# Layer 0 attention: the mixing of one group of heads moved ahead of the scores of a later group in TensorE's order

## The chip, the core and the metric

The kernel runs on one core of one Trainium2 chip. The core has five engines that each work through their own list of instructions in order and meet at semaphores: TensorE (PE in the profile; its weight loads are shown apart as PEld), VectorE (DVE), ScalarE (ACT), GpSimd (POOL) and SyncE (SP), which only starts transfers. The metric is the device time of one execution in microseconds: the median of three runs.

## The reference

The program is a stack of four layers of attention and experts over `x` of 8 sequences x 128 tokens x 256 features. The change touches only the attention of layer 0. What it computes:

```python
ln_out = _ln(hidden_states, ln_w, ln_b)
q  = _ln(fp8_linear(ln_out, wq,  ...))      # 16 heads of 128, self attention
k  = _ln(fp8_linear(ln_out, wk,  ...))      #  8 heads
v  =     fp8_linear(ln_out, wv,  ...)
core = _gqa(q, k, v)
qx = _ln(fp8_linear(ln_out, wqx, ...))      # 16 heads, cross attention
kx, vx = split(cond @ w_kv_x.T); kx = _ln(kx)
xout = _gqa(qx, kx, vx)
catq = _div_clamp_fp8(concatenate([core, xout]), proj_smooth)
out  = catq @ wproj.T * (proj_in_scale * proj_w_scale)

def _gqa(q, k, v):                          # each key head serves two query heads
    scores = einsum('bsghd,btgd->bghst', q, k) / sqrt(128)
    return einsum('bghst,btgd->bsghd', softmax(scores), v)
```

Here `_ln` is a normalisation over the 128 features of a head, and `_div_clamp_fp8` rounds to the values of an 8-bit float. Everything else of the four layers stays as it is.

## The kernel before

`layer0_attention` does the work in two passes over the 8 sequences, 16 tiles in all (`b` from 0 to 15): tiles 0 to 7 are the cross attention, tiles 8 to 15 the self attention. A tile has 8 units of work in the order k0, q0, k1, q1, v0, q2, v1, q3. A unit is 512 columns, that is four heads. The four units q0 to q3 (`a` from 0 to 3) each become one *group*: scores, softmax and mixing of four heads. So there are 64 groups.

A unit passes through a chain of small steps on four engines: `project` on TensorE (L456 for keys and values of the first pass, L466 for all others), squares on ScalarE (L818), their sum on VectorE (L666), the power -1/2 on GpSimd (L948), the product on VectorE (L674, `normalise`), `turn` on TensorE (L475, four transposes), and the copy of the turned block with scale and bias on ScalarE (L832 writes `q_t`, L837 writes `k_t`). A group then goes on: `score` on TensorE (L484, reads `q_t` and `k_t`), `row_max` on VectorE (L679), exponentials on ScalarE (L846), inverse of the row sum on VectorE (L683), `scale_probs` on ScalarE (L890), `turn_probs` on TensorE (L492), `keep_probs` on ScalarE (L853, writes `probs_t`), `mix` on TensorE (L501, reads `probs_t` and `values`), `round_mixed` on VectorE (L689, L638 to L644) and GpSimd (L920, L924, writes `cat`), `project_out` on TensorE (L512). ScalarE's copy of v into `values` is L824.

The order in which an engine does all this is written out by `march` (L163). Time is cut into steps, eight to a tile, and each function has a list of steps at which it is due, relative to its tile; a late due time reaches into the next tile. In each step `march` runs through its list of functions in the order of the list and calls those that are due. So the list sets the order within a step, and every engine has its own list. The lists are the whole plan: nothing else decides what stands behind what.

On TensorE `score` is due 4 steps and `mix` 8 steps behind the projection of its unit. Query units are at steps 1, 3, 5 and 7, so both fall on odd steps, and the two of one step belong to different groups: with the scores of group n goes the mixing of group n-2. On ScalarE, in the even step before, `keep_turned` (L832) writes the `q_t` that these scores need, and directly behind it `keep_probs` (L853) writes the `probs_t` that this mixing needs.

Of the kernel before, what the change touches and what calls it, by code (L numbers as in the profile page):

```python
# [162 lines left out]
def march(vts, steps, work):  # L163

    last = max(s for _, due in work for s in due)
    for g in range(vts * steps + last):
        for function, due in work:
            for k, s in enumerate(due):
                b, left = divmod(g - s, steps)
                if left == 0 and 0 <= b < vts:  # L170
                    function(b, k)
# [19 lines left out]
def layer0_attention(nc, top, res, w, before):  # L191


    PASSES, VTS = 2, 2 * TILES
    UNITS = [("k", 0), ("q", 0), ("k", 1), ("q", 1), ("v", 0), ("q", 2), ("v", 1), ("q", 3)]
    STEPS = len(UNITS)
# [8 lines left out]
    with phase_memory(nc, "l0a", res.given_back) as mem:  # L205
# [114 lines left out]
        at_norm, at_plain, at_query = NORMED, PLAIN, QUERY  # L320

        def later(due, n):
            return [s + n for s in due]
# [7 lines left out]
        F_TILE = VTS - 1  # L331
        F_ROWS_TILE, F_ROWS = VTS - 2, [8, 11, 12]
        F_TURN = [12, 13]
# [3 lines left out]
        def in_tile(tile, function, due):  # L337
            def at_step(b, k):
                if b == tile:
                    function(k)  # L340
            return at_step, due
# [49 lines left out]
        def _(pe):  # L391
# [136 lines left out]
            def first_up(k):  # L528
# [9 lines left out]
                for c in range(KC):  # L538
# [1 line left out]
                                   start=(c == 0), stop=(c == KC - 1))  # L540
                mm.then_inc(res.first_up_made, 1)

            march(VTS, STEPS, [(turn_probs, later(at_query, 7)), (score, later(at_query, 4)),
                               (mix, later(at_query, 8)), in_tile(F_TILE, turn_first, F_TURN),
                               in_tile(F_TILE, first_up, F_UP), (project_out, later(at_query, 11)),
                               (turn, later(at_norm, 3)), (project, range(STEPS)),
                               in_tile(0, centre_first, [0]), in_tile(0, centre_next, [1, 3, 5])])
# [2 lines left out]
        def _(v):  # L550
# [142 lines left out]
            def add_to_x(b, _):  # L693
                projected_out.wait(v, projected_out.at(b, NA))
                xt = res.x[:, b % TILES, :]
                v.scalar_tensor_tensor(xt, out_bank[:, 0:D], out_scale[:, 0:1], xt, ALU.mult, ALU.add)\
                 .then_inc(x_done.sem, 1)
                if b >= TILES:
                    token_moments(v, res, res.x, [b - TILES])
# [210 lines left out]
        def _(g):  # L910
# [60 lines left out]
            def first_rstd(_):  # L971
                g.wait_ge(f_var_ready, 1)
                g.tensor_tensor(f_rstd[:], f_var[:], res.minus_half[:, 0:4], ALU.pow).then_inc(f_rstd_ready, 1)
# [2789 lines left out]
```

## Time and profile before

| | |
|---|---|
| median of 3 runs | 1504.31 us (1501.78 to 1506.41) |
| the profiled execution | 1502.7 us |
| its span | 1500.9 us |
| PE, PEld, DVE, ACT, POOL busy in the span | 96%, 69%, 58%, 51%, 35% |
| granted TensorE clock, mean | 0.994 of full speed |

The span is the time from the first to the last instruction of the profiled execution; 1.8 us of its time lie around it. Busy time is the sum of the instructions of an engine. The ends of matmuls are modelled, so PE's busy share tells little of whether it had to wait; the idle time ahead of its weight loads (PEld) tells more. In a timeline row the columns are start, duration, engine, line, operation, output and inputs with their shapes, the number of instructions merged in the row, and in brackets the idle time of that engine just before and who ended it. The layer 0 attention takes the span from about 32 us to about 461 us.

### The profile page before, as it was taken

To read this page: it belongs to the slowest core of one execution; us is meant where nothing else is said; L and a number is where in the kernel's file an instruction comes from. 1 tells how busy PE (TensorE), PEld (TensorE's weight loads), DVE (VectorE), ACT (ScalarE), POOL (GpSimd) and SP (SyncE) were. 2 spreads that over 40 slices of the span, in tenths; PEclk is the share of its full clock that TensorE was granted. 3 is DMA by queue.
4 is the path that set the end of the run, shared out by engine and by line. 5 is a ranking of instruction groups with operands and counts; after the bars stand their busy time and mean duration, and the time that the engine had idled before them with its cause. 6 is when DMAs were issued, how large, how long until landed. Compare 5 with 4: busy or idle time off the path is not lost. (4 is left out here: it accounts for less than half of the span.)

```text
span 1500.9 us, 22370 instructions
## 1 busy us (share of the span) xinstructions
PE 1437.8 (96%) x7006; PEld 1040.2 (69%) x7006; DVE 877.0 (58%) x1923; ACT 768.6 (51%) x2123; POOL 526.4 (35%) x522
## 2 busy tenths in 40 slices
PE   6999999999989999999999999999997999999998
PEld 5677777788875555557878888866764666665656
DVE  5798988899875242333464545455677555553322
ACT  5888888999982211110234444444357655553210
POOL 2767677877761000000533333322111333321000
PEclk9999999999999999999999999999999999999999
DMA  5301000200006511112100000000232000011120
GB/s 204 118 6 64 5 5 1 97 1 1 2 1 265 180 53 49 49 50 91 67 1 1 0 1 1 15 15 6 102 150 97 1 1 1 1 30 43 47 69 17
DMA packets 21880, 71.67 MB, mean 48 GB/s; under 512 B 3922, under 2 KB 6354, under 8 KB 19076
## 3 DMA queue, kind: packets, MB, share of 16 engines
q1 hardware_dynamic: 13556, 57.38, 10.4%
q10 hardware_dynamic: 8208, 12.87, 2.8%
q8 instruction: 58, 0.95, 0.3%
q14 instruction: 58, 0.48, 0.1%
HBM read 69.01 MB, written 1.22 MB: 47 GB/s over the span
## 5 line engine op out<-in xcount | busy, mean ns | idle before, releaser
L1282 ACT ACTIVATE l0f_silu<-bank 128x512 f32<-128x512 f32 x48 | 28.5, 597 | 198.9 <-PE bank L1206 183.0
L948 POOL TENSOR_TENSOR l0a_head_rstd<-l0a_head_var,all_minus_half 128x4 f32<-128x4 f32 x96 | 99.6, 1042 | 18.2 <-DVE l0a_head_var L666 18.2
L1385 DVE TENSOR_TENSOR l0f_product<-l0f_silu,bank 128x512 f32<-128x512 f32 x48 | 32.9, 687 | 124.3 <-ACT l0f_silu L1282 124.2
L920 POOL TENSOR_TENSOR l0a_stepped<-l0a_y,l0a_m 128x512 f32<-128x512 bf16 x64 | 73.8, 1153 | 89.1 <-DVE l0a_m L644 87.5
L484 PEld LDWEIGHTS bank<-l0a_k_t,l0a_q_t 128*128 128x128 f32 x512 | 63.7, 191 | 39.7 <-ACT l0a_q_t L832 35.3
L846 ACT ACTIVATE l0a_work<-bank,l0a_neg_max 128x128 f32<-128x128 f32 x256 | 90.3, 372 | 1.2 <-DVE l0a_neg_max L679 1.2
L1218 PEld LDWEIGHTS bank<-all_weights_a,l0f_hidden 128*128 128x128 f32 x384 | 72.9, 190 | 25.3 <-issue 17.0
L1814 DVE TENSOR_TENSOR all_weights_a<-bank,all_cols 128x512 f32<-128x512 f32 x64 | 43.9, 690 | 77.6 <-PE bank L1649 46.2
L1218 PE MATMUL bank<-all_weights_a,l0f_hidden 128*128 128x256 f32 x384 | 88.9, 379 | 0.0
L2407 PE MATMUL bank<-l3a_f_xn_t,all_weights_b 128*128 128x512 f32 x192 | 86.2, 594 | 0.0
L890 ACT ACTIVATE l0a_work<-l0a_work,l0a_row_inv 128x128 f32<-128x128 f32 x256 | 82.4, 411 | 6.2 <-DVE l0a_row_inv L683 5.9
L924 POOL TENSOR_TENSOR l0a_cat<-l0a_stepped,l0a_m 128x512 fp32r<-128x512 f32 x64 | 79.3, 1239 | 10.2 <-issue 7.9
L484 PE MATMUL bank<-l0a_k_t,l0a_q_t 128*128 128x128 f32 x512 | 71.6, 283 | 9.4 <-ACT l0a_q_t L832 8.7
L1997 ACT ACTIVATE l1a_work<-bank,l1a_exp_bias,l1a_q_scale 128x128 f32<-128x128 f32 x128 | 56.8, 454 | 41.9 <-DVE l1a_exp_bias L1880 41.9
L2713 POOL TENSOR_TENSOR l3a_probs<-l3a_probs,l3a_row_inv 128x512 f32<-128x512 f32 x32 | 33.3, 1039 | 126.6 <-DVE l3a_row_inv L2514 126.6
L674 DVE TENSOR_TENSOR l0a_work<-bank,l0a_head_rstd 128x512 f32<-128x512 f32 x96 | 65.1, 678 | 16.0 <-POOL l0a_head_rstd L948 15.8
L666 DVE TENSOR_REDUCE l0a_head_var<-l0a_squares 128x4 f32<-128x516 f32 x96 | 65.6, 683 | 7.5 <-ACT l0a_squares L818 6.3
L818 ACT ACTIVATE l0a_squares<-bank 128x512 f32<-128x512 f32 x96 | 58.0, 604 | 23.1 <-DVE l0a_head_var L666 14.6
L512 PE MATMUL bank<-l0a_wp_high,l0a_cat 128*128 128x256 f32 x256 | 69.4, 305 | 0.0
L475 PE MATMUL bank<-all_ident,l0a_work 128*128 128x128 f32 x384 | 59.0, 276 | 8.3 <-DVE l0a_work L674 8.1
L501 PE MATMUL bank<-l0a_probs_t,l0a_values 128*128 128x256 f32 x256 | 66.0, 380 | 0.2 <-ACT l0a_probs_t L853 0.2
L512 PE MATMUL bank<-l0a_wp_low,l0a_cat 128*128 128x256 f32 x256 | 63.6, 281 | 0.0
(443 smaller groups left out, 3760.3 us busy)
## 6 DMA issues: line engine op xcount, KB each, us to landing
l0f_spread<-l0f_weights ACTq DMA_DIRECT2D x32, 192.0 KB, 2.7
all_weights_a<-in_l_w_q SPq DMA_DIRECT2D x2, 2048.0 KB, 13.8
l0f_spread<-l0f_weights ACTq DMA_DIRECT2D x32, 128.0 KB, 2.8
all_weights_b<-in_l_e_gate_up SPq DMA_DIRECT2D x1, 3200.0 KB, 10.4
all_weights_b<-in_l_e_gate SPq DMA_DIRECT2D x1, 3072.0 KB, 10.0
all_weights_a<-in_l_e_up SPq DMA_DIRECT2D x4, 768.0 KB, 6.7
all_weights_a<-in_l_e_down SPq DMA_DIRECT2D x1, 3072.0 KB, 15.2
l3a_spread<-l3f_weights SPq DMA_DIRECT2D x10, 256.0 KB, 3.4
```

What stands on the lines that cost most here:

```text
L484: mm = pe.matmul(score_bank[:, h * P:(h + 1) * P], q_t[:, h * P:(h + 1) * P], k_t[:, a // 2, g * P:(g + 1) * P], start=True, stop=True)
L501: mm = pe.matmul(mix_bank[:, half * 2 * P:(half + 1) * 2 * P], values[:, a // 2, g * P:(g + 1) * P], probs_t[:, half * 2 * P:(half + 1) * ...
L512: mm = pe.matmul(out_bank[:, 0:D], cat[:, a % 2, h * P:(h + 1) * P], part[:, a * HU + h, :], start=(a == 0 and h == 0 and n == 0), stop=(a ...
L666: v.tensor_reduce(head_var[:, m % 2, :], squares[:], X, ALU.add).then_inc(var_ready.sem, 1)
L674: v.tensor_tensor(heads(norm_rows[:, m % 2, :]), heads(bank_of(b, NORMED[n])), along(head_rstd[:, m % 2, :], P), ALU.mult).then_inc(norm_d ...
L846: done = act.activation(probs[:, a % 2, h * P:(h + 1) * P], score_bank[:, h * P:(h + 1) * P], ACT.Exp, bias=neg_max[:, a, h:h + 1], accum_ ...
L890: done = act.activation(pr, pr, ACT.Copy, scale=row_inv[:, a, h:h + 1])
L920: done = g.tensor_tensor(stepped[:, 0:n], value, step, ALU.add)
L924: return g.tensor_tensor(out, stepped[:, 0:n], step, ALU.subtract)
L948: g.tensor_tensor(head_rstd[:, m % 2, :], head_var[:, m % 2, :], res.minus_half[:, 0:HU], ALU.pow)\
L1218: mm = pe.matmul(down_banks[t // 2][:, (t % 2) * D:(t % 2 + 1) * D], hidden[:, n % 2, t * P:(t + 1) * P], w_down[:, j, :], start=(j == 0 a ...
L2407: mm = pe.matmul(bank[:], w_gate_up[:, c, i * (NCH - 1) * P + col:i * (NCH - 1) * P + col + P], f_xn_t[:, c, h * HALF:(h + 1) * HALF], sta ...
```

## The change

In TensorE's list the entry for `mix` stands ahead of that for `score`, where it stood behind it:

```diff
-            march(VTS, STEPS, [(turn_probs, later(at_query, 7)), (score, later(at_query, 4)),
-                               (mix, later(at_query, 8)), in_tile(F_TILE, turn_first, F_TURN),
+            march(VTS, STEPS, [(turn_probs, later(at_query, 7)), (mix, later(at_query, 8)),
+                               (score, later(at_query, 4)), in_tile(F_TILE, turn_first, F_TURN),
                                in_tile(F_TILE, first_up, F_UP), (project_out, later(at_query, 11)),
                                (turn, later(at_norm, 3)), (project, range(STEPS)),
```

No instruction is added or removed, no due step changes, and the lists of the other engines are the same.

On TensorE, in a step of the first pass in which a key block is turned as well (L456 is a projection of the cross attention, L484 the scores, L501 the mixing, L475 the turn, L466 a projection of queries):

```order
 L456 MATMUL bank<-l0a_wkx,l0a_ctx_t 128x512 [waits l0a_kx_ready,l0a_ctx_in,l0a_norm_done]
 L456 MATMUL bank<-l0a_wkx,l0a_ctx_t 128x512
-L484 MATMUL bank<-l0a_k_t,l0a_q_t 128x128 [waits l0a_exp_done,l0a_turned_out]
-L484 MATMUL bank<-l0a_k_t,l0a_q_t 128x128 x3
-L501 MATMUL bank<-l0a_probs_t,l0a_values 128x256 [waits l0a_mixed_read,l0a_values_done,l0a_probs_t_ready]
-L501 MATMUL bank<-l0a_probs_t,l0a_values 128x256
+L501 MATMUL bank<-l0a_probs_t,l0a_values 128x256 [waits l0a_mixed_read,l0a_values_done,l0a_probs_t_ready]
+L501 MATMUL bank<-l0a_probs_t,l0a_values 128x256
+L484 MATMUL bank<-l0a_k_t,l0a_q_t 128x128 [waits l0a_exp_done,l0a_turned_out]
+L484 MATMUL bank<-l0a_k_t,l0a_q_t 128x128 x3
 L475 MATMUL bank<-all_ident,l0a_work 128x128 [waits l0a_turned_out,l0a_norm_done]
 L475 MATMUL bank<-all_ident,l0a_work 128x128 x3
```

The two mixing matmuls, with their wait for `probs_t`, moved ahead of the four of the scores, with their wait for `q_t`. The turn and the projection keep their places behind the pair.

On TensorE, in a step of the second pass in which no key block is turned:

```order
 L466 MATMUL bank<-l0a_wk_high,l0a_xq 128x512
 L466 MATMUL bank<-l0a_wk_low,l0a_xq 128x512
-L484 MATMUL bank<-l0a_k_t,l0a_q_t 128x128 [waits l0a_exp_done,l0a_turned_out]
-L484 MATMUL bank<-l0a_k_t,l0a_q_t 128x128 x3
-L501 MATMUL bank<-l0a_probs_t,l0a_values 128x256 [waits l0a_mixed_read,l0a_values_done,l0a_probs_t_ready]
-L501 MATMUL bank<-l0a_probs_t,l0a_values 128x256
+L501 MATMUL bank<-l0a_probs_t,l0a_values 128x256 [waits l0a_mixed_read,l0a_values_done,l0a_probs_t_ready]
+L501 MATMUL bank<-l0a_probs_t,l0a_values 128x256
+L484 MATMUL bank<-l0a_k_t,l0a_q_t 128x128 [waits l0a_exp_done,l0a_turned_out]
+L484 MATMUL bank<-l0a_k_t,l0a_q_t 128x128 x3
 L466 MATMUL bank<-l0a_wq_high,l0a_xq 128x512 [waits l0a_w_low,l0a_quant_done,l0a_values_done]
 L466 MATMUL bank<-l0a_wq_low,l0a_xq 128x512
```

The same swap; here the query projection stands directly behind the pair. It occurs in 62 places in all: the first two groups of scores have no mixing beside them, and the last two mixings no scores.

On ScalarE, whose order is the same in both kernels, an even step and the odd step behind it (L846 exponentials, L832 `q_t`, L853 `probs_t`, L890 the scaling of the probabilities, L824 `values`, L818 squares):

```order
L846 ACTIVATE l0a_work,l0a_row_sum<-bank,l0a_neg_max 128x128 x3
L832 ACTIVATE l0a_q_t<-bank,l0a_q_affine 128x512 [waits l0a_scored,l0a_turned]
L853 ACTIVATE l0a_probs_t<-bank 128x512 [waits l0a_mixed,l0a_probs_turned]
L890 ACTIVATE l0a_work<-l0a_work,l0a_row_inv 128x128 [waits l0a_inv_ready]
L890 ACTIVATE l0a_work<-l0a_work,l0a_row_inv 128x128 x3
L824 ACTIVATE l0a_values<-bank 128x512 [waits l0a_mixed,l0a_projected]
L818 ACTIVATE l0a_squares<-bank 128x4x128 [waits l0a_var_ready,l0a_projected]
```

What TensorE's mixing waits for (L853) is written directly behind what its scores wait for (L832).

## Rows read from the trace of the kernel before

**Rows 1.** The page, part 1: busy us, share of the span, instructions.
```profile
PE 1437.8 (96%) x7006; PEld 1040.2 (69%) x7006; DVE 877.0 (58%) x1923; ACT 768.6 (51%) x2123; POOL 526.4 (35%) x522
```

**Rows 2.** Windows, second pass: span, PE, PEld, DVE, ACT, POOL, clock, DMA, GB/s.
```profile
299.00:400.00 101.00, 97.92 (x618) 82.53 (x617) 91.15 (x194) 92.72 (x296) 77.94 (x81) 1.00 0.01 1
```

**Rows 3.** Waits of TensorE's weight loads, first pass: us, times, longest.
```profile
PEld bank L484 <- ACT l0a_q_t L832: 21.3, 32, 2.6
PEld bank L484 <- issue: 3.8, 16, 0.2
```

**Rows 4.** The same view, 245 to 456 us, second pass.
```profile
PEld bank L484 <- ACT l0a_q_t L832: 14.0, 26, 1.2
```

**Rows 5.** Timeline, first pass, a group whose scores find their input ready.
```profile
139.06 0.80 ACT L832 ACTIVATE l0a_q_t<-bank,l0a_q_affine 128x512 f32<-128x512 f32 x1
...
139.72 0.62 ACT L853 ACTIVATE l0a_probs_t<-bank 128x512 f32<-128x512 f32 x1
140.12 0.19 PEld L484 LDWEIGHTS bank<-l0a_k_t,l0a_q_t 128*128 128x128 f32 x1 [0.24 <-ACT l0a_q_t L832]
...
140.55 0.86 PEld L484 LDWEIGHTS bank<-l0a_k_t,l0a_q_t 128*128 128x128 f32 x7 [0.24 <-issue]
...
141.33 0.73 PEld L501 LDWEIGHTS bank<-l0a_probs_t,l0a_values 128*128 128x128 f32 x4
```

**Rows 6.** Timeline, first pass, a group whose scores wait.
```profile
100.39 0.79 ACT L832 ACTIVATE l0a_q_t<-bank,l0a_q_affine 128x512 f32<-128x512 f32 x1
...
101.05 0.61 ACT L853 ACTIVATE l0a_probs_t<-bank 128x512 f32<-128x512 f32 x1
101.23 0.63 PEld L484 LDWEIGHTS bank<-l0a_k_t,l0a_q_t 128*128 128x128 f32 x5 [1.25 <-ACT l0a_q_t L832]
```

**Rows 7.** Timeline, ScalarE, first pass, between two `q_t`.
```profile
149.23 0.60 ACT L824 ACTIVATE l0a_values<-bank 128x512 f32<-128x512 f32 x1 [1.05 <-PE bank L501]
150.09 0.60 ACT L818 ACTIVATE l0a_squares<-bank 128x512 f32<-128x512 f32 x1 [0.27 <-PE bank L466]
```

**Rows 8.** Waits, 32 to 456 us, of ScalarE's copy of v.
```profile
ACT l0a_values L824 <- PE bank L501: 6.9, 8, 1.1
```

**Rows 9.** Timeline, TensorE's weight loads, one tile of the second pass.
```profile
350.79 0.97 PEld L484 LDWEIGHTS bank<-l0a_k_t,l0a_q_t 128*128 128x128 f32 x8 [0.64 <-ACT l0a_q_t L832]
...
355.31 0.46 PEld L475 LDWEIGHTS bank<-all_ident,l0a_work 128*128 128x128 f32 x4
...
361.30 0.42 PEld L475 LDWEIGHTS bank<-all_ident,l0a_work 128*128 128x128 f32 x4 [0.23 <-DVE l0a_work L674]
363.04 1.09 PEld L484 LDWEIGHTS bank<-l0a_k_t,l0a_q_t 128*128 128x128 f32 x8
...
367.71 0.42 PEld L475 LDWEIGHTS bank<-all_ident,l0a_work 128*128 128x128 f32 x4 [0.40 <-DVE l0a_work L674]
...
373.90 0.42 PEld L475 LDWEIGHTS bank<-all_ident,l0a_work 128*128 128x128 f32 x4
375.68 0.41 PEld L484 LDWEIGHTS bank<-l0a_k_t,l0a_q_t 128*128 128x128 f32 x3 [0.62 <-ACT l0a_q_t L832]
```

**Rows 10.** Timeline, ScalarE, the same tile.
```profile
356.09 0.80 ACT L832 ACTIVATE l0a_q_t<-bank,l0a_q_affine 128x512 f32<-128x512 f32 x1
...
362.00 0.78 ACT L832 ACTIVATE l0a_q_t<-bank,l0a_q_affine 128x512 f32<-128x512 f32 x1
362.68 0.59 ACT L853 ACTIVATE l0a_probs_t<-bank 128x512 f32<-128x512 f32 x1
...
374.83 0.80 ACT L832 ACTIVATE l0a_q_t<-bank,l0a_q_affine 128x512 f32<-128x512 f32 x1
```

**Rows 11.** Timeline, VectorE: a row maximum of the same tile, then the stage's end.
```profile
353.62 0.68 DVE L679 TENSOR_REDUCE l0a_neg_max<-bank 128x4 f32<-128x512 f32 x1
...
434.88 0.69 DVE L679 TENSOR_REDUCE l0a_neg_max<-bank 128x4 f32<-128x512 f32 x1 [1.43 <-PE bank L484]
436.42 0.69 DVE L674 TENSOR_TENSOR l0a_work<-bank,l0a_head_rstd 128x512 f32<-128x512 f32 x1 [0.85 <-POOL l0a_head_rstd L948]
```

## The prediction

> **What bounds the kernel now.** I read the page first. TensorE is busy for 96% of the span, far ahead of the others [rows 1], but the ends of its matmuls are modelled, so this does not say that it never waits. I read therefore the waits of its weight loads, in each half of the layer 0 attention. What it waits for there is above all one thing: the scores (L484) wait for `q_t`, 32 times and 21.3 us in the first pass [rows 3], 26 times and 14.0 us in the second [rows 4]. The mixing (L501) is no entry of that size: it always came behind the scores, and its input was there. The reader should see that the change moves exactly these two.
>
> Then I took single groups from the timeline. In the first pass they are of two kinds. In 16 groups the array is still at work when the scores' first weights are loaded: the load at 140.12 is followed by the second only at 140.55, after 0.24 us of "issue" [rows 5], and the waits view counts 16 such gaps [rows 3]. TensorE is the late one here. In the others (32 less 16, less the first two groups, which have no mixing: 14) TensorE stands idle, 1.25 us at 101.23 [rows 6], until `q_t` is written. ScalarE, which writes it, had itself waited for TensorE before: 1.05 us for the mixing and 0.27 us for the projection of the same step [rows 7]. So TensorE and ScalarE form a ring, with no slack in it. In the second pass VectorE (91.15 of 101 us) and ScalarE (92.72 of 101 us) are nearly full as well [rows 2], and TensorE also waits for VectorE's `l0a_work` ahead of two turns of a tile, 0.23 and 0.40 us [rows 9]. There is slack there.
>
> **The change, part by part.** Nothing is added or removed; 62 pairs are swapped. Three things follow.
>
> First, TensorE now stops for `probs_t` instead of `q_t`, and everything behind it in its queue (scores, turn, projection, the next transposes, `project_out`) waits too. ScalarE writes `probs_t` directly behind `q_t`: `q_t` ends at 100.39 + 0.79 = 101.18, the scores' load starts at 101.23, and `probs_t` ends at 101.05 + 0.61 = 101.66 [rows 6]. With the same 0.05 us behind it the mixing starts at 101.71: **0.48 us more idle time**. In a group of the first kind `probs_t` ends at 139.72 + 0.62 = 140.34; the mixing's load could start at 140.39 and its matmul some 0.11 us later (seven loads of the scores take 0.86 us in rows 5, so 0.12 each), at 140.50, while the array is busy until 140.55 [rows 5]. **It pays nothing.** In the six groups of the second pass that do not wait, `probs_t` ends at 362.68 + 0.59 = 363.27 [rows 10], against a load at 363.04 [rows 9]: 0.28 us later, less 0.12 us by which that group's loads were held up by the busy array (1.09 against 0.97 us for the eight loads), so **0.16 us**.
>
> Second, the scores end later still, by the mixing ahead of them: 0.73 us of loads [rows 5], together about 1.2 us. VectorE takes the row maximum 353.62 - (350.79 + 0.97) = 1.9 us behind the last load of the scores, of which some 0.2 us is the last matmul [rows 9, 11]: 1.7 us of slack cover the 1.2 us in the steady second pass. I count nothing there. At the end of the stage the cover is gone: VectorE itself waits 1.43 us for the scores at 434.88, and the next thing it does waits 0.85 us for GpSimd [rows 11]. So of 1.2 us between 0.35 and 1.2 are paid once by the last groups. I take 1.0, because behind the very last scores hardly anything else is left to hide them.
>
> Third, the mixing ends 0.4 us earlier than now (0.48 us later start, but 0.9 us of scores no longer ahead). Eight times ScalarE's copy of v waits for it, 6.9 us in all [rows 8]. But directly behind the copy ScalarE waits again, for the projection that stands behind both [rows 7], and that one comes later, not earlier. So this gain turns into a longer wait one instruction on: nothing.
>
> A rule of the Trainium skill would soften the first point. The trace first: in the 1.25 us of idle time at 101.23 no weight load of the work behind (mixing, projection) went ahead of the waiting scores [rows 6]; TensorE's loads stood still. "TensorE: Matmul & The Clock Gate", in the section on what each phase is for, says that TensorE's queue may pull a weight load ahead of matmuls in flight. By that rule the first load of the scores could be done while the mixing waits, and by the trace it cannot; the rival below has the price.
>
> The sum. First pass: 14 groups pay 0.48 us. Since ScalarE's last wait before such a group is for TensorE [rows 7], a delay of TensorE comes back with the next `q_t`, and the payments add up. I leave out the first of them, at the filling of the stage, where ScalarE is the late one: 13 x 0.48 = **6.2 us**. Second pass: a tile lasts 375.68 - 350.79 = 24.89 us [rows 9] and pays 3 x 0.48 + 0.16 = 1.6 us. Against this stand the slacks of its four turns: 0.23 and 0.40 us of waiting for VectorE [rows 9], and the time from turn to `q_t`, which is 0.70 us where ScalarE waits for the turn (361.30 to 362.00), 0.78 at 355.31 and 0.93 at 373.90, so 0.08 and 0.23 us [rows 9, 10]. 1.6 less 0.94 leaves 0.66; I take 0.6 us a tile, and four tiles of this even kind (from 300 to 400 us). In the tiles before and behind them TensorE's waits for VectorE are longer and swallow it. **2.4 us.** The end of the stage: **1.0 us.** Together 9.6 us. The stages behind start from the end of this one and are only shifted. The profiled execution of 1502.7 us becomes 1512.3; it lies 1.6 us below the median, and the median of 1504.31 becomes **1514**.
>
> Bounds: nothing at all if each delay falls into slack (1504), and from above every group in full: 14 + 26 groups at 0.48, 16 + 6 at 0.28 (the later load, whatever the array does), and 1.2 at the end, together 26.6 us (1531). The value taken lies nearer the lower end because the 16 groups are held by the busy array and the second pass by VectorE.
>
> **The rivals.**
> *It is hidden (no change).* VectorE and ScalarE are over 90% busy in the second pass [rows 2] and TensorE has slack there; if the first pass behaves so too, the delays never close the ring. It speaks against it that ScalarE waits for TensorE right before the waits of TensorE [rows 7]. The 2.4 us go and the 6.2 us shrink to less than half: 1504 to 1508. Chance 0.12.
> *Every delay is paid, and late scores cost too.* VectorE falls behind at the row maxima, its lateness comes back through `l0a_work` to the turns, and the slack at the two turns is no more. For it speaks that VectorE is as full as ScalarE; against it the 1.7 us of cover. Between the forecast's 9.6 and 26.6 us, near the upper end: about 1526. Chance 0.13.
> *Faster.* The place is ScalarE's copy of v: with the mixing 0.4 us earlier in 8 groups, and the mixed heads earlier at `round_mixed`, the ring loses 8 x 0.4 = 3.2 us, at most the 6.9 us [rows 8]. It decides only if ScalarE's next wait, for the projection, were not behind it; that is in the trace [rows 7]. 1497 to 1501. Chance 0.03.
> *TensorE loads ahead.* If weights of the scores are loaded while the mixing waits, each paying group gives back one load, 0.12 us of its 0.48: a quarter of the 8.6 us of both passes, 2.2 us, 1512. This is the mechanism of the page named above. Chance 0.04.
>
> **How the numbers follow.** The forecast has 0.68 and a range of its own from 1509 to 1519: the first pass alone, with two or three of its groups absorbed, gives 5 us, and one us more for each of the four tiles gives 13.6. The whole range takes in most of the no-change and part of the full-payment case: 1507 to 1523. A difference under 0.3% (4.5 us) cannot be told from no change. Faster by more than that: 0.02 (the upper half of that rival). Within 0.3%: the hidden case and the lower half of the faster one, with a little of the forecast's lower edge, 0.13. Slower: 0.85.
>
> **What would show it.** Right: TensorE's waits at L484 for `q_t` vanish, and waits at L501 for ScalarE's L853 stand in their place, some 40 of them and about 0.5 us longer each; the loads at L501 start 0.05 us behind the end of L853; ScalarE's wait at L824 for L501 shrinks and the one behind it at L818 grows. The period of a tile grows by 1 to 2 us around 90 to 115 us, by 0.5 to 0.7 us from 300 to 400 us, and not where TensorE is late throughout (139 to 153 us). The stage ends about 10 us later and all behind is shifted unchanged. Wrong: `probs_t` ready before TensorE arrives in most groups (then the change costs nothing), or VectorE waiting at L679 in the steady tiles (then it costs more), or the difference lying outside layer 0's attention.

## The result and the profile after

The changed kernel takes **1514.02 us** (median of 5 runs, 1509.39 to 1516.63), the kernel before 1504.31 us (median of 5 runs beside them, 1501.78 to 1506.41): ratio 1.0066, 95% interval 1.0043 to 1.0089, so slower by 6.5 to 13.4 us. Forecast were 1514 us and slower. The profiled execution took 1515.11 us, with a span of 1513.3 us.

Part 1 of the page after, beside [rows 1], tells next to nothing: every engine does the same work.

```profile
PE 1437.7 (95%) x7004; PEld 1041.7 (69%) x7006; DVE 876.5 (58%) x1923; ACT 766.7 (51%) x2123; POOL 526.1 (35%) x522
```

The waits of TensorE's weight loads after, 32 to 466 us (waited for, us in total, times, longest), answer to [rows 3, 4]:

```profile
PEld bank L501 <- ACT l0a_probs_t L853: 59.9, 63, 1.9
...
PEld bank L484 <- ACT l0a_q_t L832: 3.8, 2, 2.6
PEld bank L475 <- DVE l0a_work L674: 3.7, 8, 1.1
```

The wait for `q_t` is gone but for the first two groups, which have no mixing beside them. The wait for `probs_t` stands in its place, in 63 of the 64 mixings. The same view for the engines around:

```profile
DVE l0a_neg_max L679 <- PE bank L484: 24.9, 29, 2.8
ACT l0a_squares L818 <- PE bank L466: 24.0, 30, 1.4
...
ACT l0a_values L824 <- PE bank L501: 0.8, 5, 0.2
```

ScalarE's wait at its copy of v shrank from 6.9 us [rows 8] to 0.8. Its wait at the squares rose to 24.0 us; the view of the kernel before, 32 to 456 us, has for the two entries that grew:

```profile
ACT l0a_squares L818 <- PE bank L466: 4.8, 19, 0.3
...
DVE l0a_neg_max L679 <- PE bank L484: 3.9, 3, 1.7
```

The pair of [rows 7] after, ScalarE between two `q_t` of the first pass. The wait moved one instruction on, from the copy to the squares:

```profile
151.72 0.60 ACT L824 ACTIVATE l0a_values<-bank 128x512 f32<-128x512 f32 x1 [0.16 <-PE bank L501]
153.48 0.60 ACT L818 ACTIVATE l0a_squares<-bank 128x512 f32<-128x512 f32 x1 [1.16 <-PE bank L466]
```

Now the single groups. The one of [rows 6] after, ScalarE:

```profile
101.84 0.80 ACT L832 ACTIVATE l0a_q_t<-bank,l0a_q_affine 128x512 f32<-128x512 f32 x1
...
102.50 0.62 ACT L853 ACTIVATE l0a_probs_t<-bank 128x512 f32<-128x512 f32 x1
```

and TensorE's loads:

```profile
103.17 0.73 PEld L501 LDWEIGHTS bank<-l0a_probs_t,l0a_values 128*128 128x128 f32 x4 [1.60 <-ACT l0a_probs_t L853]
103.92 1.08 PEld L484 LDWEIGHTS bank<-l0a_k_t,l0a_q_t 128*128 128x128 f32 x8
```

The mixing's load starts at 103.17, which is 0.05 us behind the end of `probs_t` (102.50 + 0.62). Measured from the start of `q_t`, TensorE goes on 1.33 us later (103.17 - 101.84), where it was 101.23 - 100.39 = 0.84: 0.49 us, as predicted (0.48). The matmuls of the same two places, before (first fence) and after (second), show the idle time of the array itself, which is shorter than that of the loads (1.25 and 1.60 us). Their ends are modelled, so these figures are rough:

```profile
101.23 1.16 PE L484 MATMUL bank<-l0a_k_t,l0a_q_t 128*128 128x128 f32 x8 [0.42 <-ACT l0a_q_t L832]
```
```profile
103.17 1.13 PE L501 MATMUL bank<-l0a_probs_t,l0a_values 128*128 128x256 f32 x4 [0.77 <-ACT l0a_probs_t L853]
```

The group of [rows 5], where the array was late, after:

```profile
142.45 0.80 ACT L832 ACTIVATE l0a_q_t<-bank,l0a_q_affine 128x512 f32<-128x512 f32 x1
...
143.12 0.62 ACT L853 ACTIVATE l0a_probs_t<-bank 128x512 f32<-128x512 f32 x1
...
143.79 0.77 PEld L501 LDWEIGHTS bank<-l0a_probs_t,l0a_values 128*128 128x128 f32 x4 [0.52 <-ACT l0a_probs_t L853]
...
143.93 1.03 PE L501 MATMUL bank<-l0a_probs_t,l0a_values 128*128 128x256 f32 x4
```

The profile puts 0.52 us of waiting down here, and yet nothing is lost: the load at 143.79 precedes the matmul by 0.14 us, because the array is still at work. An idle time of the loads is not yet an idle time of the array.

One tile of the second pass after, beside [rows 9, 10]. ScalarE:

```profile
356.80 0.80 ACT L832 ACTIVATE l0a_q_t<-bank,l0a_q_affine 128x512 f32<-128x512 f32 x1
357.47 0.62 ACT L853 ACTIVATE l0a_probs_t<-bank 128x512 f32<-128x512 f32 x1
...
382.43 0.80 ACT L832 ACTIVATE l0a_q_t<-bank,l0a_q_affine 128x512 f32<-128x512 f32 x1
```

TensorE's loads:

```profile
358.14 0.73 PEld L501 LDWEIGHTS bank<-l0a_probs_t,l0a_values 128*128 128x128 f32 x4 [0.90 <-ACT l0a_probs_t L853]
358.89 1.08 PEld L484 LDWEIGHTS bank<-l0a_k_t,l0a_q_t 128*128 128x128 f32 x8
...
362.65 0.46 PEld L475 LDWEIGHTS bank<-all_ident,l0a_work 128*128 128x128 f32 x4
...
368.85 0.46 PEld L475 LDWEIGHTS bank<-all_ident,l0a_work 128*128 128x128 f32 x4
```

The tile lasts 382.43 - 356.80 = 25.63 us, where it lasted 24.89. The waits of 0.23 and 0.40 us ahead of the two turns [rows 9] are gone: they were the slack, and it is used up. The window of 101 us shows no engine as full as in [rows 2] (columns as there):

```profile
306.00:407.00 101.00, 93.48 (x599) 79.89 (x598) 88.97 (x191) 88.48 (x282) 77.65 (x80) 1.00 0.00 1
```

The stage's last instruction before (first fence) and after (second) puts the loss inside the stage at 9.74 us; the 4.82 us ahead of it are alike:

```profile
460.50 0.48 DVE L696 SCALAR_TENSOR_TENSOR all_x<-bank,l0a_out_scale,all_x 128x256 f32<-128x256 f32 x1 [4.82 <-PE bank L512]
```
```profile
470.24 0.48 DVE L696 SCALAR_TENSOR_TENSOR all_x<-bank,l0a_out_scale,all_x 128x256 f32<-128x256 f32 x1 [4.82 <-PE bank L512]
```

How far the changed kernel is behind at each `q_t` (start after less start before, from the timelines of both) shows where it is lost, in us:

| group | 4th | 7th | 8th | 11th | 15th | 16th to 19th | 20th | 28th | 32nd, end of first pass | 34th | 35th | 45th | 49th | 53rd | 57th | 58th | 62nd | 64th | stage end | program end |
|---|---|---|---|---|---|---|---|---|---|---|---|---|---|---|---|---|---|---|---|---|
| behind | 0.1 | 0.5 | 1.0 | 1.5 | 2.9 | 3.4 | 3.8 | 4.6 | 6.0 | 6.6 | 5.3 | 6.1 | 6.9 | 7.6 | 8.3 | 8.8 | 8.0 | 8.6 | 9.7 | 12.4 |

In the first pass it grows in steps, most of them just under 0.5 us, and stands still from the 16th to the 19th group (132 to 152 us of the kernel before). At the beginning of the second pass 1.2 us are given back, then it grows by 0.73 us a tile, and behind the 58th group another 0.8 us are given back before the end takes 1.7 us. The first giving back is an idle time of ScalarE ahead of L890, where it waited 1.40 us for VectorE in the kernel before and waits no more after (there the instruction starts at 260.38, with no such wait). Before:

```profile
255.05 1.28 ACT L890 ACTIVATE l0a_work<-l0a_work,l0a_row_inv 128x128 f32<-128x128 f32 x4 [1.40 <-DVE l0a_row_inv L683]
```

The last 2.7 us do not belong to the stage. They arise at one place, the beginning of the experts of layer 0. TensorE's load at L1161 before and after:

```profile
497.49 0.42 PEld L1161 LDWEIGHTS bank<-all_ident,l0f_rows 128*128 128x128 f32 x4 [2.01 <-issue]
```
```profile
508.41 0.64 PEld L1161 LDWEIGHTS bank<-all_ident,l0f_rows 128*128 128x128 f32 x4 [3.19 <-issue]
```

and the 20 us from there on, before and after (columns as in [rows 2]; the seventh is the granted clock):

```profile
497.49:517.49 20.00, 19.28 (x60) 12.16 (x61) 5.22 (x10) 5.43 (x8) 0.00 (x0) 0.83 0.38 113
```
```profile
508.41:528.41 20.00, 19.29 (x57) 12.07 (x58) 5.17 (x10) 4.43 (x8) 0.00 (x0) 0.74 0.28 79
```

At L1161 the changed kernel is 10.9 us behind instead of 9.7, since the idle time there is 3.19 us instead of 2.01. Then the granted clock has a stretch at its lower level (1.2 instead of 2.4 GHz): 20 us at a mean of 0.83 are 20 x 0.17 x 2 = 6.8 us at half clock before, 20 us at 0.74 are 10.4 us after, and it falls 1.3 us further behind.

### The profile page after: what moved, and what is told of

The parts are those of the page before. It is cut to its first block and busy times, and to the rows that moved or that the text cites. A ratio compares the mean times of both kernels' runs of the same rounds, so it can differ in the third digit from the quotient of the medians.

```text
span 1513.3 us, 22368 instructions
## 1 busy us (share of the span) xinstructions
PE 1437.7 (95%) x7004; PEld 1041.7 (69%) x7006; DVE 876.5 (58%) x1923; ACT 766.7 (51%) x2123; POOL 526.1 (35%) x522
## 3 DMA queue, kind: packets, MB, share of 16 engines
q1 hardware_dynamic: 13556, 57.38, 10.2%
## 5 line engine op out<-in xcount | busy, mean ns | idle before, releaser
L501 PE MATMUL bank<-l0a_probs_t,l0a_values 128*128 128x256 f32 x256 | 70.6, 398 | 27.2 <-ACT l0a_probs_t L853 27.2
L846 ACT ACTIVATE l0a_work<-bank,l0a_neg_max 128x128 f32<-128x128 f32 x256 | 90.2, 372 | 3.3 <-DVE l0a_neg_max L679 3.3
L501 PEld LDWEIGHTS bank<-l0a_probs_t,l0a_values 128*128 128x128 f32 x256 | 43.9, 189 | 63.3 <-ACT l0a_probs_t L853 59.9
L890 ACT ACTIVATE l0a_work<-l0a_work,l0a_row_inv 128x128 f32<-128x128 f32 x256 | 83.0, 422 | 2.6 <-DVE l0a_row_inv L683 2.2
L924 POOL TENSOR_TENSOR l0a_cat<-l0a_stepped,l0a_m 128x512 fp32r<-128x512 f32 x64 | 78.5, 1227 | 10.2 <-issue 7.6
L818 ACT ACTIVATE l0a_squares<-bank 128x512 f32<-128x512 f32 x96 | 58.2, 606 | 35.8 <-PE bank L466 24.0
L484 PEld LDWEIGHTS bank<-l0a_k_t,l0a_q_t 128*128 128x128 f32 x512 | 67.1, 191 | 7.0 <-ACT l0a_q_t L832 3.8
L484 PE MATMUL bank<-l0a_k_t,l0a_q_t 128*128 128x128 f32 x512 | 67.7, 275 | 2.1 <-ACT l0a_q_t L832 2.1
```

The lines of the kernel that those rows point to most:

```text
L484: mm = pe.matmul(score_bank[:, h * P:(h + 1) * P], q_t[:, h * P:(h + 1) * P], k_t[:, a // 2, g * P:(g + 1) * P], start=True, stop=True)
L501: mm = pe.matmul(mix_bank[:, half * 2 * P:(half + 1) * 2 * P], values[:, a // 2, g * P:(g + 1) * P], probs_t[:, half * 2 * P:(half + 1) * ...
L846: done = act.activation(probs[:, a % 2, h * P:(h + 1) * P], score_bank[:, h * P:(h + 1) * P], ACT.Exp, bias=neg_max[:, a, h:h + 1], accum_ ...
L890: done = act.activation(pr, pr, ACT.Copy, scale=row_inv[:, a, h:h + 1])
L924: return g.tensor_tensor(out, stepped[:, 0:n], step, ALU.subtract)
```

## The experiments

All kernels compute the whole program. "Stage" is how much later than in the profile of before the last instruction of layer 0's attention starts, counted from the first `q_t` of each profile (their beginnings differ by up to 3 us); the columns behind the ratio are in us, from one profile each. The medians stand against those of the kernel before, run beside them: 1503.78 (31 runs) for the first four rows, 1503.84 (23) for the next three, 1505.73 (7) for the three behind them, and 1504.31 (5) for the last.

| kernel | median us (runs) | ratio [95%] | end of first pass | stage | rest of the program |
|---|---|---|---|---|---|
| mixing first and `probs_t` ahead of `q_t` | 1503.44 (12) | 1.0002 [0.9988, 1.0016] | +0.1 | +0.2 | -1.3 |
| `probs_t` ahead of `q_t` alone | 1509.23 (10) | 1.0037 [1.0021, 1.0052] | +6.1 | +7.1 | +1.7 |
| mixing first in the first pass | 1510.55 (6) | 1.0047 [1.0030, 1.0064] | +6.2 | +5.6 | +0.8 |
| mixing first in the second pass | 1508.02 (10) | 1.0026 [1.0012, 1.0040] | +0.1 | +4.5 | +1.5 |
| mixing first in the 16 array-late groups | 1505.26 (1) | | +0.6 | +0.6 | -1.1 |
| `probs_t` still earlier | 1503.08 (12) | 0.9994 [0.9981, 1.0007] | -0.2 | +0.4 | -1.4 |
| mixing last | 1506.37 (10) | 1.0018 [1.0004, 1.0032] | +2.0 | +3.5 | -1.3 |
| `probs_t` later | 1540.72 (4) | 1.0234 [1.0199, 1.0269] | +20.4 | +35.8 | +1.4 |
| before, again | 1504.18 (1) | | +0.1 | +0.3 | -1.5 |
| after, again | 1518.09 (1) | | +6.1 | +9.9 | +2.6 |
| after | 1514.02 (5) | 1.0066 [1.0043, 1.0089] | +6.0 | +9.7 | +2.7 |

**Both lists swapped.** TensorE mixes first as in the changed kernel, and ScalarE writes `probs_t` ahead of `q_t`:

```diff
-                               (keep_values, later(at_plain, 1)), (keep_turned, later(at_norm, 3)),
-                               (prepare, range(STEPS)), (keep_probs, later(at_query, 7)), (square, at_norm),
+                               (keep_values, later(at_plain, 1)), (keep_probs, later(at_query, 7)),
+                               (keep_turned, later(at_norm, 3)), (prepare, range(STEPS)), (square, at_norm),
```

> The changed kernel, and on ScalarE probs_t (L853) is written ahead of q_t and k_t (L832, L837). Theory (TensorE pays because probs_t is finished 0.48 us behind q_t): with probs_t first the mixing starts before the scores did and its 0.76 us cover the writing of q_t, so the loss of 9.7 us goes; a pair ends about 0.1 us earlier than before the change: 1498 to 1504 us, end of the attention stage not later than before. Rival (the scores standing 0.76 us later is what costs): they still end late, so at least half of the loss stays: 1509 or more.

1503.44 us, no difference from before. ScalarE in the group of [rows 6]:

```profile
101.91 0.61 ACT L853 ACTIVATE l0a_probs_t<-bank 128x512 f32<-128x512 f32 x1
102.38 0.80 ACT L832 ACTIVATE l0a_q_t<-bank,l0a_q_affine 128x512 f32<-128x512 f32 x1
```

and TensorE's loads there:

```profile
102.57 0.73 PEld L501 LDWEIGHTS bank<-l0a_probs_t,l0a_values 128*128 128x128 f32 x4 [0.79 <-ACT l0a_probs_t L853]
103.32 0.96 PEld L484 LDWEIGHTS bank<-l0a_k_t,l0a_q_t 128*128 128x128 f32 x7
```

The mixing starts 0.05 us behind `probs_t` and the scores 0.75 us later still, 0.14 us behind the end of `q_t` (103.18): TensorE's second input becomes ready while it works on the first. Measured from the moment at which ScalarE starts on the first of the two inputs, the scores' first load comes 1.41 us later here (103.32 - 101.91), 0.84 us in the kernel before and 2.08 us in the changed one (103.92 - 101.84). So the scores are still later than before, by 0.57 us where TensorE would have waited, and it costs 0.2 us in the whole stage. The mixing's place is not the cause of the loss, and neither is this much lateness of the scores; the other 0.67 us of it is not tested here.

**ScalarE's list alone.** Scores first on TensorE as before, `probs_t` ahead of `q_t` on ScalarE (the edit above without the change itself).

> TensorE's order as before the change (scores, then mixing), but on ScalarE probs_t (L853) is written ahead of q_t and k_t. Theory: what TensorE waits for first is again written second, 0.48 us later, and costs about the same as the change: 1510 to 1517. Rival (lateness of the scores by the mixing ahead of them costs): here they are late by 0.48 us only, so half the loss or less: 1505 to 1508.

1509.23 us, slower, stage 7.1 us behind. TensorE waits at the scores again, more often and longer than before (32 and 26 times, 35.3 us in [rows 3, 4]):

```profile
PEld bank L484 <- ACT l0a_q_t L832: 61.9, 63, 2.6
```

Of the four combinations of two orders, the two with the same order on both engines are alike and the two with opposite orders lose 7.1 and 9.7 us in the stage. The scores are late by only 0.49 us here, less than with both lists swapped, and yet it costs: what costs is that TensorE stops for what is written second. The loss comes from the mismatch. Up to the 58th group the two mismatched kernels are equally far behind (8.6 us here, 8.8 in the changed kernel, from the first `q_t`); their difference arises behind it, where this one ends at 7.1 and the changed kernel at 9.7. There the changed kernel's scores are later by the mixing ahead of them, and VectorE waits 1.25 us for the last of them where it waits 0.48 us here. That the late scores make this difference is read from the two traces; no run changes them alone.

**Each pass alone.** `mix` stands in the list twice, once ahead of `score` for the tiles of one pass, once behind it for those of the other:

```diff
+            def in_pass(core, function):
+                def at_step(b, a):
+                    if b // TILES == core:
+                        function(b, a)
+                return at_step, later(at_query, 8)
...
+            march(VTS, STEPS, [(turn_probs, later(at_query, 7)), in_pass(0, mix), (score, later(at_query, 4)),
+                               in_pass(1, mix), in_tile(F_TILE, turn_first, F_TURN),
```

That is the mixing first in the first pass; with `in_pass(1, mix)` ahead and `in_pass(0, mix)` behind it is first in the second.

> The mixing stands ahead of the scores only for the tiles of the first pass (0 to 7). Theory: 6.0 us at the end of the first pass as in the changed kernel, and perhaps a part of it given back in the second pass, whose VectorE has slack from it: 1508 to 1511, the stage ends 4.5 to 6 us later than before. Rival (the two passes are not additive): the whole is given back in the second pass, 1504 to 1506.

> The mixing stands ahead of the scores only for the tiles of the second pass (8 to 15). Theory: nothing until 245 us, then 0.7 us for each of the four even tiles and about 1 us at the stage's end: the stage ends 3 to 4.5 us later, 1507 to 1509. Rival (VectorE covers it all in the second pass): 1504 to 1505.

The first pass alone is 6.2 us behind at its end and 5.6 at the end of the stage (1510.55 us); the second alone loses 4.5 us (1508.02 us). Together they make 10.1, against 9.7 for both: the two add up. In the first of them the lag still grows to 6.8 us at the 34th group and falls to 5.5 at the 35th, where nothing is swapped any more: that is the giving back at the start of the second pass, and from there to the end it stays within 0.1 us.

**Only the groups where the array is late.** The mixing is first only beside the 16 groups of [rows 5]'s kind:

```diff
+            AHEAD = [4, 5, 8, 9, 12, 15, 16, 17, 18, 19, 20, 21, 23, 24, 25, 27]
...
+                    if (NA * b + a + 2 in AHEAD) == ahead:
+                        function(b, a)
```

> The mixing stands ahead of the scores only beside the 16 groups of the first pass whose scores found their input ready (the array was the late one). Theory (the busy array hides the later input): nothing, the attention stage ends within 0.5 us of before. Rival (the 0.28 us by which the load comes later are paid each time): the stage ends 4 to 5 us later.

0.6 us behind, just above the 0.5 expected, where the 14 other groups make up most of the 6.0 us of the first pass. The 0.6 us are not spread over the 16 groups: 0.50 us of them arise between the 19th and the 20th `q_t`, and the other 15 groups lose 0.1 us together. The split into two kinds holds, with one exception. At that place ScalarE's squares (L818 before, L826 in this kernel, whose lines are shifted) wait longer for VectorE, before (first fence) and here (second):

```profile
157.06 0.60 ACT L818 ACTIVATE l0a_squares<-bank 128x512 f32<-128x512 f32 x1 [1.08 <-DVE l0a_head_var L666]
```
```profile
160.71 0.60 ACT L826 ACTIVATE l0a_squares<-bank 128x512 f32<-128x512 f32 x1 [1.59 <-DVE l0a_head_var L674]
```

VectorE does the same work there without a pause in both, 0.5 us later here. The kernel with both lists swapped loses the same 0.5 us at this place and gets it back by the end of the pass. Both have late scores, which is the likely reason; that path is argued, and no run takes it apart.

**`probs_t` still earlier.** Mixing first, and ScalarE writes `probs_t` at the head of its step, ahead of the exponentials:

```diff
-            march(VTS, STEPS, [(exponentials, later(at_query, 5)), (scale_probs, later(at_query, 6)), (scale_input, [1, 3, 7]),
+            march(VTS, STEPS, [(keep_probs, later(at_query, 7)),
+                               (exponentials, later(at_query, 5)), (scale_probs, later(at_query, 6)), (scale_input, [1, 3, 7]),
...
-                               (prepare, range(STEPS)), (keep_probs, later(at_query, 7)), (square, at_norm),
+                               (prepare, range(STEPS)), (square, at_norm),
```

> The changed kernel, and on ScalarE probs_t (L853) is written at the head of the step, ahead of the exponentials (L846), so that the mixing's 0.76 us can lie beside the exponentials and TensorE waits for q_t alone. Theory: q_t is written 0.48 us later where ScalarE is late, but no mixing stands behind the scores, so the path to the turn and the projection is 0.2 to 0.3 us shorter in each of the 14 waiting groups of the first pass: the stage ends 2 to 5 us earlier than before, 1498 to 1502. Rival (ScalarE waits for the turned probabilities at the head of the step, in which TensorE has just come from its projection): the exponentials come later by that wait, no gain or a loss, 1504 to 1512.

1503.08 us, not to be told from before; the expected 2 to 5 us did not come. TensorE's waits for `q_t` fell from 35.3 us in 58 to 8.1 us in 17, and others took their place. The largest waits of TensorE's loads and of ScalarE, 32 to 461 us (before, these two were 10.8 us in 23 and 12.9 us in 24):

```profile
PEld bank L475 <- DVE l0a_work L674: 20.5, 36, 1.4
ACT l0a_squares L818 <- DVE l0a_head_var L666: 19.5, 28, 1.8
```

Now TensorE and ScalarE both wait more for VectorE. An input that is ready earlier than needed gives only what the next engine has to spare, here 0.2 us in the first pass.

**The mixing last in the step**, behind the turn and the projection:

```diff
-                               (score, later(at_query, 4)), in_tile(F_TILE, turn_first, F_TURN),
+            march(VTS, STEPS, [(turn_probs, later(at_query, 7)), (score, later(at_query, 4)),
+                               in_tile(F_TILE, turn_first, F_TURN),
...
-                               (turn, later(at_norm, 3)), (project, range(STEPS)),
+                               (turn, later(at_norm, 3)), (project, range(STEPS)), (mix, later(at_query, 8)),
```

> TensorE's mixing stands last in its step, behind turn and projection (ScalarE as before). Theory (what costs is TensorE's stop for probs_t with work queued behind it, and ScalarE then waits for turn and projection): both of these come 0.76 us earlier, and probs_t is long written, so ScalarE's waits for the turn of the keys and for the projection shrink: the stage ends 3 to 8 us earlier, 1496 to 1501. Rival (ScalarE's copy of v, four steps of a tile apart, waits for the mixing of the same step, and its squares stand behind that copy): it waits 1 us longer once a tile in both passes, and the gain is lost, 1503 to 1510.

1506.37 us, 2.5 us over before, the stage 3.5 us behind: the rival's case. ScalarE's copy of v now pays for the late mixing, 19.7 us in 14 waits where it was 6.9 in 8 [rows 8]:

```profile
ACT l0a_values L824 <- PE bank L501: 19.7, 14, 2.0
```

**`probs_t` later.** The changed kernel with ScalarE's `keep_probs` behind the squares, one instruction of 0.60 us further back:

```diff
-                               (prepare, range(STEPS)), (keep_probs, later(at_query, 7)), (square, at_norm),
+                               (prepare, range(STEPS)), (square, at_norm), (keep_probs, later(at_query, 7)),
```

> The changed kernel, and on ScalarE probs_t (L853) is written behind the squares (L818) of its step, about 0.6 us later still in the steps that have squares, which are those before the third and fourth group of a tile. Theory (the loss is TensorE's stop for probs_t, carried round the ring): the third and fourth groups of each tile pay 1.1 us in place of 0.48, and also where the array was the late one: 16 groups of the first pass pay about 0.5 us more, so its end lies 12 to 16 us behind the kernel before, where the changed kernel lay 6.0 us behind; the whole 1520 to 1532. Rival (late scores cost, whatever TensorE stops for): the same growth is smaller, since VectorE has 1 us of slack left: 1514 to 1518.

1540.72 us, and the stage 35.8 us behind: the direction was right, the size far off. The waits, 32 to 495 us:

```profile
PEld bank L501 <- ACT l0a_probs_t L853: 87.0, 63, 3.3
DVE l0a_neg_max L679 <- PE bank L484: 54.4, 52, 3.5
```

ScalarE in one group of it, where the array had been the late one, and TensorE's load behind it:

```profile
169.34 0.80 ACT L832 ACTIVATE l0a_q_t<-bank,l0a_q_affine 128x512 f32<-128x512 f32 x1
171.02 0.60 ACT L818 ACTIVATE l0a_squares<-bank 128x512 f32<-128x512 f32 x1 [0.88 <-PE bank L456]
171.52 0.59 ACT L853 ACTIVATE l0a_probs_t<-bank 128x512 f32<-128x512 f32 x1
```
```profile
172.16 0.73 PEld L501 LDWEIGHTS bank<-l0a_probs_t,l0a_values 128*128 128x128 f32 x4 [2.00 <-ACT l0a_probs_t L853]
```

From the start of `q_t` to the end of `probs_t` it takes 171.52 + 0.59 - 169.34 = 2.77 us, where it was 1.29 in the changed kernel (357.47 + 0.62 - 356.80). The expectation took the squares as 0.6 us of work. But the squares have an input of their own: they wait for a projection on TensorE, here 0.88 us, and now `probs_t` waits behind them. The step back put a product of TensorE ahead of what TensorE stops for.

In the timelines the squares stand between the two inputs in 30 of the 62 groups, in the other 32 nothing has changed. In those 30 `probs_t` ends 0.48 to 1.48 us later than in the changed kernel, once 2.4 us (that time the squares waited for VectorE). The sum is 14.4 us in the first pass and 12.0 in the second. The additional loss is 20.4 - 6.0 = 14.4 us in the first pass and 35.8 - 9.7 = 26.1 us in the stage, so 11.7 in the second. Every further microsecond of lateness was thus paid in nearly full length, also in groups where the array had been the late one, while the first 0.48 us were free there. Two stretches of 3.4 us at the lower clock fall into the stage of this profile and may carry up to 3.4 us of it.

**Before and after once more**, for the 2.7 us behind the stage.

> The kernel before, a second profile. Theory (the attention stage is repeatable, and what differs from run to run are the stretches at half TensorE clock): the time from the first q_t to the end of the stage within 0.3 us of the first profile, the rest within 1.5 us.

> The changed kernel, a second profile. Theory: from the first q_t to the end of the stage 9.7 us longer than before, within 0.3 us; the further 2.7 us behind the stage in the first profile belong to a longer stretch at half clock there and are not there again when that stretch is short. Rival: they come from the change, and are there again.

The window behind the stage's end (columns as in [rows 2]) of before again, first fence, and after again, second fence:

```profile
464.00:523.00 59.00, 56.94 (x173) 29.35 (x172) 25.69 (x77) 16.00 (x25) 1.02 (x1) 0.97 0.72 279
```
```profile
473.80:535.00 61.20, 57.83 (x168) 30.66 (x167) 24.70 (x75) 16.00 (x25) 1.01 (x1) 0.92 0.69 267
```

Half clock takes 59 x 0.03 x 2 = 3.5 us in the first and 61.2 x 0.08 x 2 = 9.8 us in the second. The rest of the program took 1.5 us less than in the first profile of before, and 2.6 us more in the changed kernel, once again. So the 2.7 us are no single accident. They go with the length of the stretch of lower clock at the start of layer 0's experts. Over all twelve profiles:

| half clock there, us | rest of the program, us | kernels |
|---|---|---|
| 0 | -1.4 | `probs_t` still earlier |
| 3.4 | -1.5 to -1.1 | both lists, 16 groups, mixing last, before again |
| 6.8 | 0, +0.8 | before, first pass alone |
| 6.8 | +1.4 to +1.7 | ScalarE's list, second pass alone, `probs_t` later |
| 10.2 | +2.6, +2.7 | after, after again |

The idle time ahead of L1161 (2.01 us before, 3.19 after) goes with the kernel as well. In the five profiles whose second pass has the orders mismatched (after twice, ScalarE's list, second pass alone, `probs_t` later) it is 3.16 to 3.37 us, in the seven others 1.84 to 2.21 us, with the first pass alone among them, whose stage ends later than that of the second pass alone. Over twelve profiles this parts the kernels without an exception, so some 1.2 us behind the stage most likely come with the change; why they do is open.

Nor are they fully in the medians: over the eight timed kernels the difference of the medians (9.7, -0.3, 5.5, 6.8, 4.2, 2.5, -0.8, 35.0 us) follows the stage (9.7, 0.2, 7.1, 5.6, 4.5, 3.5, 0.4, 35.8 us) within 1.7 us, and in seven of the eight it is not above it. How long this stretch is varies between executions of one program. Every profile whose stage ends 4.5 us or more behind has 6.8 or 10.2 us of it, and of the others only the first of before; whether a late start makes it longer, or chance does, is open.

## Why the prediction was right, point by point

*The time and the sign.* 1514 forecast, 1514.02 measured. The median grew by 9.7 us, the sum was 9.6. The stage itself grew by 9.74 us in the profile. That the sign and the mechanism came out is shown by the runs; that the figure came out to a tenth is luck. The five executions spread over 7.2 us, terms of up to 1.7 us cancel inside the stage, and 2.7 us in the profile had no term. The terms one by one:

*First pass, 6.2 us.* Measured 6.03 us at its last group, 6.1 in the second profile and 6.2 in the kernel with that pass alone. The unit of 0.48 us is in the trace (1.33 against 0.84 us from `q_t` to TensorE's next load), and the still stretch, forecast from 139 to 153 us, is in the table. The count of 13 equal payments is not quite what happened: eleven steps of 0.41 to 0.50 us, and 0.8 us in three smaller ones (0.09, 0.32, 0.37). The last of these belongs to the 19th group, one of the 16 that were to pay nothing; the 15 others pay next to nothing. And where the prediction says that TensorE stands idle for 1.25 us, this is its loads; the array's own gap in that row is 0.42 us.

*Second pass, 0.6 us a tile, 2.4 us.* Measured 25.63 - 24.89 = 0.74 us a tile. The working had given 0.66 and I rounded down; the slacks of 0.23 and 0.40 us are used up entirely. But the pass has more to it: at its start the changed kernel gets 1.2 us back (6.6 behind at the 34th group, 5.3 at the 35th), where ScalarE and TensorE waited for VectorE and can come later at no cost. I had let those tiles swallow their own delays, but not give back earlier ones. Against that, the tiles from there to the 58th group lose 3.5 us (5.3 to 8.8) and not 2.4: more of them pay than the four that I counted. From 6.0 at the end of the first pass to 8.8 us at the 58th group it is 2.8 us against 2.4 (+0.6, -1.2, +3.5): the sum came out well because the giving back and the payments that I did not count cancel.

*The stage's end, 1.0 us.* 0.9 (8.8 to 9.7), but again as a difference: 0.8 us are given back up to the 62nd group (8.0), and 1.7 us are lost from there to the end. VectorE waits there 2.77 us at L679 instead of 1.43 [rows 11]:

```profile
444.26 0.69 DVE L679 TENSOR_REDUCE l0a_neg_max<-bank 128x4 f32<-128x512 f32 x1 [2.77 <-PE bank L484]
```

*Late scores, nothing.* Right in the sum, but one sign was misjudged. I wrote that VectorE waiting at L679 in the steady tiles would mean that it costs more. It does wait there, 24.9 us in 29 waits against 3.9 in 3, in the tile above too:

```profile
360.20 0.69 DVE L679 TENSOR_REDUCE l0a_neg_max<-bank 128x4 f32<-128x512 f32 x1 [0.46 <-PE bank L484]
```

Yet the kernel with only ScalarE's list swapped loses as much up to the 58th group and has 9.5 us in 12 waits there. VectorE is not what closes the ring in these tiles: when TensorE and ScalarE slow down by 0.74 us a tile, VectorE has less to do per microsecond (88.97 of 101 us, it was 91.15), arrives earlier relative to them, and waits. Its wait is an effect of the loss, not a part of it. Late scores are not free everywhere: the 0.5 us at the 19th group and the stage's end are where they probably cost, so a small part of the rival *Every delay is paid, and late scores cost too* is in the result.

*The earlier mixing, nothing.* Right: L824's wait went from 6.9 to 0.8 us and L818's from 4.8 to 24.0. The reverse experiment, with the mixing last, shows the limit of the argument: a mixing that is later than before does cost, 19.7 us of waiting at L824 and 3.5 us in the stage.

*All behind only shifted.* Wrong in the profile, by 2.7 us, for which the prediction had no term: 1.2 us of idle time ahead of L1161 and a longer stretch of lower clock. The profiled execution was forecast at 1512.3 us and took 1515.1.

*The rivals.* Hidden: no, by 9.7 us. Every delay paid: no, 15 of the 16 array-late groups pay next to nothing. Of the signs, the waits at L501 were to be some 40 and are 63, because the view counts those of the array-late groups and of the six short delays of the second pass too. Faster by way of the copy of v: no, the next wait took it. TensorE loads ahead: the rule of the Trainium skill ("TensorE: Matmul & The Clock Gate", on what each phase is for) is that a weight load may be pulled ahead of matmuls in flight; read widely, it would let the scores' load go ahead of the waiting mixing. In the trace the scores' first load stands 0.75 us behind the mixing's first (103.92 against 103.17), in the other groups 0.75 to 0.80 us, and no wait for `probs_t` has one inside it. The rule speaks of matmuls in flight, and here the load in front stands at a semaphore, so the trace does not contradict it; it only does not apply. The time of 1512 us that the rival gave would not have been told from the forecast by the median alone; the loads tell it.

## What to carry to other kernels

When two engines hand each other work in a ring without slack, write the inputs in the order in which they are consumed: either order was worth 1503 to 1504 us here, as long as both engines had the same one, and a mismatch cost up to 0.50 us in each group whose consumer stood idle. Look first for what the consumer will find missing, and count only places where the array itself is idle: a wait ahead of a weight load that ended while the array still worked cost next to nothing here, and an engine that merely waits more may do so because the ring has become slower. Slack is used once: 62 delays of 0.48 us (30 us) cost 9.7 us in the stage, 30 further ones of 26 us together cost 26 us. And before an instruction is put ahead of a critical one, ask what it waits for itself: the squares brought their own wait for TensorE with them.

## What the runs showed of the hardware

- Two instructions of ScalarE that follow one another overlap: `q_t` takes 0.80 us and `probs_t` starts 0.66 to 0.67 us after it (357.47 against 356.80). Written second, an input is thus 0.48 us later, less than the 0.62 us of its own duration.
- A weight load that stood at a semaphore held all loads behind it: 63 waits and 59.9 us at L501 in the changed kernel, with no load of the scores inside.
- The granted clock falls to its lower level for 3.4 to 10.2 us at the same place of the program in eleven of twelve profiles, around the idle time of TensorE ahead of L1161. Among executions of one and the same kernel the length changed from 6.8 to 3.4 us (clock 0.83 over 20 us in one, 0.97 over 59 us in the other), and the rest of the program by 1.5 us. What sets the length is open. Where the idle time was 3.16 to 3.37 us the stretch was 6.8 or 10.2 us, where it was 1.84 to 2.21 us the stretch was none, 3.4 or 6.8 us; no run changes that idle time alone.
